# Two 3x3 convolutions with group norms on one core: thirteen input chunks split ahead of the first convolution, fifteen warm-up matmuls, three low parts on GpSimd

## What is computed

```python
def _gn(v, G=8, eps=1e-5):
    g = v.reshape(B_, G, C_ // G, H_, W_)
    return ((g - mean(g)) / sqrt(var(g) + eps)).reshape(v.shape)

# layer 0: one set of taps per image
z = einsum('bchw,oc->bohw', gn(x), rot_w) + rot_b            # batch-normalized, averaged over pixels
angle = tanh(sum(angles)) * pi / 4
w = real(ifftn(w_fft * exp(-2j * pi * cos(angle) * fsum)))[mid]
x = x + conv3x3_zero_padded(gn(x), w)                         # 8 images as 8 groups
# layer 1
x = x + real(fft2(einsum(Lw, ifft2(gn(x)))))                  # circular 3x3 convolution
```

## Time and profile before

| | |
|---|---|
| median of 3 runs (lowest to highest) | 1762.68 us (1761.88 to 1762.94) |
| the profiled execution | 1762.14 us |
| its span | 1760.3 us |
| TensorE matmul busy | 1653.9 us, 94% |
| VectorE busy | 1381.3 us, 78% |
| ScalarE busy | 1169.0 us, 66% |
| GpSimd busy | 130.9 us, 7% |
| mean DMA rate over the span | 232 GB/s |

### The profile page before, as it was taken

How to read it: one execution, slowest core, us unless ns; L and a number is a source line. 1 busy time by engine, 2 the same in 40 slices (tenths; PEclk the granted TensorE clock), 3 DMA queues, 4 the chain that set the end, 5 groups by cost and what they waited for, 6 DMA issues and landing times.

```text
span 1760.3 us, 65152 instructions
## 1 busy us (share of the span) xinstructions
PE 1653.9 (94%) x29295; PEld 1263.6 (72%) x29295; DVE 1381.3 (78%) x2202; ACT 1169.0 (66%) x1050; POOL 130.9 (7%) x383
## 2 busy tenths in 40 slices
PE   5888888688799999999999999999999999999999
PEld 5888878554466667887788668866886678666755
DVE  5998999789988888888887888788878888878600
ACT  6888788579666666666666666666666666666444
POOL 0000000032200020002000200020002000100100
PEclk9999899889899999999999999999999999999999
DMA  9999999565456666656665666666666665666245
GB/s 385 421 421 422 422 421 421 210 187 163 121 162 206 199 194 213 216 188 202 214 206 195 202 218 195 205 196 212 196 203 208 202 209 194 209 196 207 110 197 205
DMA packets 101979, 411.65 MB, mean 234 GB/s; under 512 B 17139, under 2 KB 19688, under 8 KB 85352
## 3 DMA queue, kind: packets, MB, share of 16 engines
q1 hardware_dynamic: 100329, 407.51, 65.9%
q10 hardware_dynamic: 735, 0.37, 0.1%
q0 software_dynamic: 672, 0.08, 0.1%
HBM read 271.83 MB, written 136.07 MB: 232 GB/s over the span
## 4 chain that ended last, share of the span: by engine, by line
PE 69%; DVE 16%; issue 8%; ACT 3%; DMA 2%; DVEq 0%; POOL 0%; SPq 0%; ACTq 0%; POOLq 0%
PE ps L459 36%; PE ps L452 32%; DVE x L737 9%; DVE x L957 2%; DVE nat L798 2%; ACT x L578 1%; DVE stats L995 1%; DMA x<-x_pix 1%; ACT x L576 1%; ACT nat L563 1%; DMA x<-wf 1%; PE ps L387 1%; DMA xin<-x_tiles 0%; PE ps L388 0%; DVE x L798 0%
## 5 line engine op out<-in xcount | busy, mean ns | idle before, releaser
L459 PE MATMUL ps<-x,wc 64*64 64x512 f16 (+2 forms) x12585 | 1159.7, 374 | 6.0 <-POOL x L715 6.0
L452 PE MATMUL ps<-nat,wc 64*64 64x512 f16 (+1 forms) x11784 | 1137.6, 377 | 15.3 <-DVE x L957 11.3
L459 PEld LDWEIGHTS ps<-x,wc 64*64 64x64 f16 x12585 | 677.6, 107 | 178.4 <-POOL x L715 7.1
L452 PEld LDWEIGHTS ps<-nat,wc 64*64 64x64 f16 x11784 | 655.9, 107 | 190.2 <-issue 33.3
L563 ACT ACTIVATE nat<-xin,gnp 128x1024 f16<-128x1024 f32 (+1 forms) x249 | 283.3, 1138 | 295.8 <-PE ps L452 284.5
L957 DVE SCALAR_TENSOR_TENSOR x<-ps,gnp,x 128x1024 f16<-128x1024 f32 (+1 forms) x264 | 333.1, 1262 | 31.2 <-ACT x L578 21.6
L593 ACT ACTIVATE outb<-ps,bias 128x1024 f32<-128x1024 f32 (+1 forms) x264 | 289.7, 1097 | 73.1 <-PE ps L459 57.5
L582 ACT ACTIVATE x<-ps,gnp 128x1024 f16<-128x1024 f32 (+1 forms) x229 | 251.0, 1096 | 118.7 <-DVE stats L995 118.4
L798 DVE SCALAR_TENSOR_TENSOR nat<-xin,gnp,nat 128x1024 f16<-128x1024 f32 (+1 forms) x249 | 313.4, 1259 | 2.0 <-ACT nat L563 1.9
L387 PE MATMUL ps<-x 128*128 128x129 f16 x2048 | 259.9, 227 | 54.2 <-DVE x L737 54.0
L737 DVE SCALAR_TENSOR_TENSOR x<-x 128x2048 bf16<-128x2048 f32 x128 | 282.8, 2287 | 19.1 <-DMA x<-wf 17.3
(11 more groups left out here) (139 smaller groups left out, 384.2 us busy)
## 6 DMA issues: line engine op xcount, KB each, us to landing
x<-x_pix SPq DMA_DIRECT2D x128, 1024.0 KB, 11.2
xin<-x_tiles SPq DMA_DIRECT2D x256, 512.0 KB, 3.8
out<-outb SPq DMA_DIRECT2D x256, 512.0 KB, 4.1
xin<-x_tiles SPq DMA_DIRECT2D x8, 192.5 KB, 2.4
out<-outb SPq DMA_DIRECT2D x8, 192.5 KB, 3.0
w<-taps_scratch SPq DMA_DIRECT2D x60, 8.0 KB, 2.9
w<-taps_scratch SPq DMA_DIRECT2D x30, 16.0 KB, 3.2
taps_scratch<-x POOLq DMA_DIRECT2D x21, 3.0 KB, 3.0
```

The lines of the kernel that those rows point to most:

```text
L452: return nc.tensor.matmul(ps[64 * kind:64 * kind + 64, bank, 0:w], lhs, planes[rows, xhl, a:a + w], start=first, stop=last)
L459: ins = nc.tensor.matmul(ps[64 * kind:64 * kind + 64, bank, done:done + part], lhs, x1[rows, xhl, z:z + part], start=first and done == 0, ...
```

## The change

Chunks 4 to 12 (`STAGED`) get a place of their own for the raw input, in `x1` where the first stage's pieces lay. SyncE loads them as soon as the first stage's last low part is made, so thirteen chunks are loaded ahead. Their high and low parts get places too: 0 to 3 in `nat`, 4 to 6 at the end of `x1`, 7 to 12 in `x1` from slot 25 (`SIX_AT`). GpSimd pads all of image 0, from the moment `gnp` is written. `hi0(0)` and `lo0(0)` go into the chain of small steps, `hi0` of 1 to 9 and `lo0` of 1 to 4, 6 and 7 follow ahead of turn 0, and in the turns the two run by tables of their own: `hi0` of 10 to 16 in turns 0 to 6, `lo0` of 9, 10 and 12 to 16 in turns 0 to 6, neither in turns 7 to 9, and from turn 10 on chunk `g + 7` again, up to chunk 37. GpSimd makes the low parts of chunks 5, 8 and 11 (`low_part`: two operations of 1024 columns). The other images' taps are sent by GpSimd behind all this. `WARM` is 15.

```diff
-TURN = (NCH // NSEVEN + 1) * NSEVEN
+STAGED = range(NX, NX + 9)
+LAP = STAGED.stop
+TURN = LAP + 3 * NSEVEN
+HI_FIRST = 10
+ON_POOL = (5, 8, 11)
+SIX_AT, STAGE_AT = 25, 6
-DVE_FIRST = 12
-WARM = 7
+WARM = 15
+def ahead_lo(g):
+    if g == 0:
+        return 9
+    return (10, 12, 13, 14, 15, 16)[g - 1] if g < 7 else ahead(g) if g + NSEVEN >= LAP + NX else None
+def ahead_hi(g):
+    if g + HI_FIRST < LAP + NX:
+        return g + HI_FIRST
+    return ahead(g) if g + NSEVEN >= LAP + NX else None
...
             for dst, src in ((cst[:, :], consts), (w132[:, :], w1band)):
                 sp.dma_start(dst, src).then_inc(late_in, 16)
+            sp.wait_ge(a_lo, B * NACH + ASLOTS)
+            for g in STAGED:
+                load_x(g)
...
-            for g in range(NX, 2 * NX):
+            for g in range(LAP, LAP + NX):
                 load_x(g)
...
-                if g + 2 * NX < ALL:
+                if LAP + NX <= g + NSEVEN + NX < TURN + NX:
+                    load_x(g + NSEVEN + NX)
+                if TURN + NX <= g + 2 * NX < ALL:
                     load_x(g + 2 * NX)
...
+                if STAGE_AT <= g < STAGE_AT + 2 * len(STAGED):
+                    lo0_made(act, NX + (g - STAGE_AT) // 2 + 1)
                 act.wait_ge(summed, g + 1)
...
-            pool.wait_ge(zve, Z_TAPS)
-            pool.wait_ge(zdma, 16 * 4)
-            for b in range(1, B):
-                taps_out(pool, b, taps_rest)
...
+            def low_part(g):
+
+                planes, a = nat_at(g)
+                pool.wait_ge(hi0_ready, g + 1)
+                link(G.tensor_scalar(x_at(g), x_at(g), gnp[:, 1, 0:1], 1.0, ALU.mult, ALU.mult))
+                G.tensor_tensor(planes[:, 1, a:a + CH], x_at(g), planes[:, 0, a:a + CH], ALU.subtract).then_inc(pool_lo, 1)
+
+            pool.wait_ge(zve, Z_GNP)
+            for g in range(LAP):
+                first_pad(g)
+            join(NX)
+            for g in range(LAP, LAP + NX):
+                first_pad(g)
+            for g in ON_POOL:
+                low_part(g)
+            join(NSEVEN)
+            pool.wait_ge(zve, Z_TAPS)
+            pool.wait_ge(zdma, 16 * 4)
+            for b in range(1, B):
+                taps_out(pool, b, taps_rest)
             for turn in range(NCH):
-                if DVE_FIRST <= turn + 9 < NCH:
+                if LAP + NX <= turn + 9 < NCH:
                     first_pad(turn + 9)
```

More of the change, by code:

```diff
@@ L216, in conv_program @@
         x_in = [sem(f"x_in{s}") for s in range(NX)]
+        x_early = [sem(f"x_early{g}") for g in STAGED]
         w_in = sem("w_in")
@@ L534, in _, with hi0 @@
                                              ACT.Identity, scale=AS).then_inc(a_hi, 1)
+            def hi0(g):
+                b, n = divmod(g, NCH)
+                w = CH if n < NFULL else EDGE
+                if g < NCH:
+                    act.wait_ge(pool_pad, g + 1)
+                else:
+                    act.wait_ge(pad_done, g + 1 - NCH)
+                if g >= LAP:
+                    act.wait_ge(pe_done, JOB0[g - (LAP if g < LAP + NSEVEN else NSEVEN if g < TURN + NX else NX)] + 1)
+                planes, a = nat_at(g)
+                nc.scalar.activation(planes[:, 0, a:a + w], x_at(g)[:, 0:w], ACT.Identity,
+                                     scale=gnp[:, 1, b:b + 1]).then_inc(hi0_ready, 1)
             act.wait_ge(zve, Z_VAR)
             nc.scalar.activation(zc[0:C, 48:64], zc[0:C, 32:48], ACT.Sqrt).then_inc(zac, 1)
+            hi0(0)
             act.wait_ge(zve, Z_BNVAR)
@@ L549, in _ @@
                                      bias=trig[:, 2 * k + 1:2 * k + 2], scale=trig[:, 2 * k:2 * k + 1]).then_inc(zac, 1)
-            def hi0(g):
-                b, n = divmod(g, NCH)
-                w = CH if n < NFULL else EDGE
-                if DVE_FIRST <= g < NCH:
-                    act.wait_ge(pool_pad, g + 1 - DVE_FIRST)
-                else:
-                    act.wait_ge(pad_done, g + 1 - (NCH - DVE_FIRST if g >= NCH else 0))
-                last = g - (NSEVEN if g < TURN + NX else NX)
-                if last >= 0:
-                    act.wait_ge(pe_done, JOB0[last] + 1)
-                planes, a = nat_at(g)
-                nc.scalar.activation(planes[:, 0, a:a + w], xin[:, g % NX, 0:w], ACT.Identity,
-                                     scale=gnp[:, 1, b:b + 1]).then_inc(hi0_ready, 1)
             def hi1(g):
@@ L594, in finish @@
                                      bias=bias[:, b % 2:b % 2 + 1], scale=1.0 / (HS * X1S)).then_inc(o_done, 1)
-            for g in range(2):
+            for g in range(1, NX):
                 hi0(g)
@@ L599, in _ @@
             load_weights(act, 0, ((0, 1), (1, 1)), w_in)
-            for g in range(2, NX):
-                hi0(g)
-            for g in range(NX, NSEVEN):
+            for g in range(NX, HI_FIRST):
                 hi0(g)
@@ L607, in _ @@
                     hi1(g)
-                if ahead(g) is not None:
-                    hi0(ahead(g))
+                if ahead_hi(g) is not None:
+                    hi0(ahead_hi(g))
                 if g < ALL and not early:
@@ L929, in by_tap @@
                 return a.unsqueeze(1).to_broadcast([n2, B, 9])
+            lo0(0)
             after_act(3)
@@ L935, in _ @@
             at(link(V.tensor_tensor(ztb, ztb, zub, ALU.add)), Z_T)
-            for g in range(NX):
-                pad(g)
             after_pe()
@@ L1107, in biased @@
                                 bias[:, 2 + b % 2:3 + b % 2], ALU.mult, ALU.add).then_inc(bias_ready, 1)
-            for g in range(2):
+            for g in range(1, NX + 1):
                 lo0(g)
@@ L1112, in _ @@
                 weights0(0, part)
-            for g in range(2, NX):
+            for g in (6, 7):
                 lo0(g)
-            for g in range(NX, NSEVEN):
-                pad(g)
-            for g in range(NX, NSEVEN):
-                lo0(g)
-            pad(NSEVEN)
             for g in range(ALL + LAG):
@@ L1146, in _ @@
                         lo1(g - 1)
-                    if ahead(g) is not None:
-                        lo0(ahead(g))
+                    if ahead_lo(g) is not None:
+                        lo0(ahead_lo(g))
                     if n == NFULL - 1:
@@ L1176 @@
 Z_FORMS = Z_WA + 3 + 4 + 1
+Z_GNP = Z_FORMS + 2
 Z_BNVAR = Z_FORMS + 3 + 10
```

61 lines of the change are left out of this document (44 added, 17 removed).

## The result

The changed kernel takes **1757.1 us** (1756.37 to 1758.23, 9 runs), the kernel before 1762.68 (1761.21 to 1764.47, 9 runs): ratio 0.9972, 95% interval 0.9962 to 0.9981. A second set of 11 runs, on the chip of experiments 6 and 7, gave 1758.2 and a ratio of 0.9980 (0.9971 to 0.9989); the median of all 20 is 1758.0. The profiled execution took 1757.1 us with a span of 1755.3, where the one of before had 1762.14.

What follows compares the result with a forecast made beforehand. Image 0 alone was taken as bound by ScalarE, then VectorE, and from 495 us TensorE is never short of work. Terms summed to -5.6 us from 1762.14, giving 1756.5, plus 0.5 for the median: 1757.0 us, range 1753.0 to 1760.8.

Steps and rivals of the forecast that it cites:

- The chain, +0.5: Small steps ahead of the weights: nothing removed, added copies and a slightly late `hi0(0)` cost 0.5 us.
- The start, -4.4: Start of the convolution: full clock from the first step and VectorE free, so chunk 0 is read 4.4 us earlier.
- Turns 7 to 9, -3.1: Image 0's turns 7 to 9: ScalarE has no `hi0`, three times 1.04 us, saving 3.1 us.
- The wait at chunk 11, -0.6: ScalarE's 0.67 us wait at chunk 11, from VectorE's full turn 10, should go: 0.6 us saved.
- Turn 31, -0.5: `lo0(38)` moves from turn 31 to 34, saving 0.5 us (0.1 to 1.2), as TensorE hides most.
- GpSimd, +2.5: GpSimd's three low parts, early in image 0: 1.0 us of lateness plus 1.5 of `lo0` waiting; ends 0 and 8.
- GpSimd was not free: Concerns the rival that GpSimd's low parts cost nothing, its term 0: 1754.5 us, 16%.
- the clock was up at the first job: Concerns the rival that the clock is down again when the convolution's first job starts: 1759.1 us, 16%.
- GpSimd holds VectorE up as well: Rival: four `lo0` wait behind GpSimd, 3.8 us and not 1.5, turns 1 to 6 become VectorE's: 1759.3 us, 16%.
- The other side: GpSimd late by far at chunk 7's copy and chunk 17's pad: break-even at 383.6, 1767.2 us if 388.2; 5%.

Runs made afterwards that it cites:

- experiments 6 and 7: Both on experiment 3's kernel. 6: other images' taps sent first, 1756.38 us; 7: work only seven chunks ahead, thirteen still loaded, 1758.43 us.
- experiment 1: The changed kernel with 7 warm-up matmuls in place of 15: 1759.56 us, ratio 0.9985.
- experiment 2: The kernel before with 15 warm-up matmuls in place of 7 and nothing else: 1762.43 us, ratio 0.9998.
- experiment 5: The changed kernel with the other images' taps sent first, as before, and GpSimd's low parts behind them: 1763.48 us, ratio 1.0000.
- experiment 3: The changed kernel with the low parts of chunks 5, 8 and 11 back on VectorE: 1756.46 us, and 1756.75 when run again.

## Why the prediction was right, and where its terms were not

The forecast of 1757.0 us was met, by 1757.1 in the first set and 1758.0 over all. The mechanisms at the start and behind GpSimd were right; that the number fits to a tenth is luck, since one term failed and others made up for it. The terms, against the table:

- *The chain, +0.5.* The first job starts at 359.29 in place of 358.65. `hi0(0)` runs at 342.06 (341.6 forecast). The warm-up, which follows the chain, starts 0.9 us later, and the gap before the first job gives 0.3 of that back. The eleven traces with the change start it between 358.75 and 360.37, 0.65 later than before on average. About right.
- *The start, -4.4.* The clock was 1.00 from the first matmul, the gap 1.50 us, and chunk 0 was read at 366.20 where 365.9 stood. From the first job that is -4.7. Right, with two things left unsaid: the term is no sum of a clock and a free VectorE but the later of the two (experiments 1 and 2), and of the clock's 2.6 us only 0.1 lasts to chunk 32 beside GpSimd's low parts (experiment 1).
- *Turns 7 to 9, -3.1: the step that failed.* The text said that TensorE's 2.6 is more than ScalarE's 2.2, "but it has two finished chunks in hand". When turn 7 came it had none: it had itself just waited 1.0 us for `lo1` (385.15), and then ran five jobs without a gap, at 2.7 us each. With every low part on VectorE the three turns (from the read of chunk 6 to that of chunk 9) take 2.71 us each: TensorE's floor, 0.5 less than before, 1.5 in all. In the changed kernel they take 2.71, 2.19 and 2.17, because ScalarE, held back by VectorE's waits for GpSimd, comes to chunks 8 and 9 some 1.5 and 1.0 us after TensorE has finished them (an estimate: 385.15 and 21 steps of 0.22 us, then 2.7 more). That is used up one turn later, when VectorE's mask of chunk 10 waits for TensorE and the turn takes 3.46 us:

```profile
395.34 0.17 DVE L1034 TENSOR_TENSOR ps<-ps,cst 128x8 f32<-128x8 f32 x1 [0.40 <-PE ps L505]
```

- *The wait at chunk 11, -0.6.* It did not go: 0.86 us in the changed kernel. From chunk 10 to 11 is 3.02 us there, 2.85 before and 2.57 with every low part on VectorE, so 0.3 were to be had.
- *Turn 31, -0.5.* From chunk 31 to 32 is 3.79 us in place of 4.90: 1.1, near the end of the bounds (0.1 to 1.2), and it is 3.79 or 3.80 in every kernel that has `lo0(38)` moved. I had thought TensorE would hide most of it on its way to the group means. That depends on the clock. From the read of chunk 31 to that matmul it is 5.36 us in the changed kernel (466.06 to 471.42), 5.96 in experiment 5, whose clock is low for longer there, and before 6.90 or, with the shorter stretch of low clock of experiment 2, 6.47. So against the profiled execution of before the turn is worth 1.5 us, of which 0.4 is the clock's.
- *GpSimd, +2.5.* The end of its work was forecast well, the copy for chunk 7 being done at 377.1 (378), partly by two errors that cancel: it began at 363.5 (362), and its scaling takes 1.11 us (1.7), its add 2.13 (2.3). `hi0(17)` at 395.68 had its pad since 390.5. The term is 2.3 us by the table and 1.4 by the medians, but of another make: not 1.0 of lateness and 1.5 of waiting, but all waiting. VectorE lost 3.65 us in three `lo0`, and was 2.9 us behind at chunk 7.

So the sum held, with a wrong term in it. Without the chain the forecast's terms make -6.1 us. The table has -5.0 for them, taken by way of experiment 3: -4.7 for the start, -1.5 and -0.3 for the work ahead, -1.1 for turn 31, +2.3 for GpSimd, and 0.3 between chunks 11 and 31 that no term had. The term that failed was 1.6 us too good, and the errors at the start and in turn 31 gave 0.9 of it back. Another 0.7 came from behind chunk 32, where no term stood (0.4 of it is the clock near the group means). The median of all 20 runs, 1758.0, shows a missing microsecond; that of the first nine did not.

Two rivals fell at once: GpSimd was not free (experiment 3), and the clock was up at the first job. Of the others, "GpSimd holds VectorE up as well" had the mechanism right and its size too (3.8 us of waiting said, 3.65 seen), and 2.3 us of it reached chunk 32. It was priced at 1759.3 because lateness was added to it, and there was none: the copy for chunk 7 was done 1.5 us before the job of chunk 6 began (377.1 and 378.64). The Trainium skill's rule in "SBUF — State Buffer", section "Who interferes with whom", is borne out on every count that these traces can show: two-input `lo0` waits (2.85 us for 1.28), and `lo1` with one input from PSUM doesn't. "The other side" had the place right and its point wrong. It put the break-even at 383.6 for the copy of chunk 7, with one microsecond lost for each late; experiment 5 has it done at 381.1 and the gain is gone. What its price left out, by the trace of experiment 5, is that the TensorE kept waiting there also lost its clock. The prediction itself took the gap before the first job as safe because it was shorter than the 3.1 us after which the clock had fallen before; it was (1.50 us, clock 1.00), but the last section has falls with waits of 2.8 and 2.5 us.

## What to carry to other kernels

Before handing a busy VectorE's work to an idle GpSimd, look at what VectorE runs in that stretch: where it has operations with both inputs in SBUF, an operation of GpSimd that reads SBUF held it up here, and the three low parts taken off it (3 x 1.28 = 3.8 us) cost it 3.65 us of waiting. The cost is not in the idle times of the profile but in the durations: compare each row with the same form elsewhere. When work is moved out of a turn, the gain is the distance to the next engine's time for that turn (here 0.5 us), unless that engine has work finished in advance, and the trace must show that it has.
